# The second row's norm moved into the first row's last attention groups, with all unit and load places set anew

## The reference

```python
x = x + attn(layernorm(x))          # 16 heads of 32, linear attention in chunks, head-wise RMS norm
x = x + mamba(ctx, layernorm(x))    # conv, 16 states per channel, scan over 512 steps, gated by silu(layernorm(x))
x = x + ffn(layernorm(x))           # ternary weights (24 blocks of 128 x 1024), 8-bit activations
```

## Time and profile before

| | |
|---|---|
| three runs, median (lowest to highest) | 954.26 us (953.02 to 956.2) |
| the profiled execution | 954.95 us, span 953.2 us |
| busy: PE, DVE, ACT, POOL | 84%, 83%, 62%, 51% of the span |
| mean granted TensorE clock | 0.912 of full speed |
| row 0, step 1, step 2, step 3, last row | 213.7, 237.1, 217.4, 192.1, 92.9 us |

### The profile page before, as it was taken

The page is one execution under the profiler, slowest core; times in us unless marked ns, Lnnn a source line. Parts: engine busy times, 40 slices in busy tenths (PEclk is TensorE's granted clock), DMA queues, the critical chain, the costliest instruction groups (busy, mean ns, idle before and its releaser), DMA issues.

```text
span 953.2 us, 11602 instructions
## 1 busy us (share of the span) xinstructions
PE 804.4 (84%) x4036; PEld 445.1 (47%) x4036; DVE 787.1 (83%) x932; ACT 591.2 (62%) x865; POOL 481.7 (51%) x283
## 2 busy tenths in 40 slices
PE   5779678657688998998989788999978899998798
PEld 1336345433453444656354344656445346664354
DVE  5899976887687888979699998697599998977874
ACT  3779889974466766545367866455266787434443
POOL 0465776885536434574446653465455655562020
PEclk9789977858789899989989999989989999999799
DMA  9668887867336443775635673665724566673000
GB/s 292 247 180 250 221 250 215 243 189 210 77 66 138 98 99 67 178 155 129 148 66 100 121 145 67 145 144 111 177 66 89 111 149 130 150 158 66 1 12 34
DMA packets 50494, 130.92 MB, mean 137 GB/s; under 512 B 7203, under 2 KB 7587, under 8 KB 50437
## 3 DMA queue, kind: packets, MB, share of 16 engines
q0 software_dynamic: 16128, 58.73, 32.5%
q1 hardware_dynamic: 34308, 71.45, 24.1%
HBM read 67.09 MB, written 4.35 MB: 75 GB/s over the span
## 4 chain that ended last, share of the span: by engine, by line
PE 48%; DVE 21%; ACT 14%; issue 7%; DMA 6%; POOL 4%; SPq 0%; DVEq 0%; POOLq 0%; ACTq 0%
PE bank L847 15%; PE bank L1056 7%; DVE W L1842 5%; PE bank L970 5%; PE bank L876 4%; DMA ACC<-W 3%; PE bank L895 3%; PE bank L1073 3%; ACT DEC L1300 3%; PE bank L954 3%; POOL W L1680 2%; DVE U L1798 2%; DMA CROW<-c_rows 2%; PE bank L915 2%; PE bank L932 2%
## 5 line engine op out<-in xcount | busy, mean ns | idle before, releaser
L1680 POOL TENSOR_TENSOR W<-W,CROW 128x1024 f32<-128x1024 f32 x128 | 322.6, 2535 | 186.4 <-DVE W L1842 166.5
L1842 DVE TENSOR_TENSOR_SCAN W<-DEC,PB 128x1024 f32<-128x1024 f32 x125 | 285.1, 2281 | 7.6 <-DMA ACC<-W 3.9
L1693 POOL DMA_DIRECT2D ACC<-W x112 | 98.8, 882 | 152.3 <-DMA ACC<-W 127.6
L1831 DVE TENSOR_TENSOR PB<-DU,PB 128x1024 f32<-128x1024 f32 x128 | 156.6, 1224 | 19.4 <-PE PB L1011 17.8
L1300 ACT ACTIVATE DEC<-DT,ACOL 128x511 f32<-128x511 f32 x250 | 160.2, 709 | 7.4 <-DVE W L1842 7.3
L1056 PE MATMUL bank<-W,ARENA 128*128 128x512 fp8e4 x512 | 128.2, 396 | 0.0
L1255 ACT ACTIVATE ARENA<-bank 128x512 f32<-128x512 f32 x56 | 32.8, 591 | 86.0 <-PE bank L847 46.6
L1056 PEld LDWEIGHTS bank<-W,ARENA 128*128 128x128 bf16 x512 | 46.2, 100 | 64.9 <-issue 22.4
L876 PE MATMUL bank<-IDF,ARENA 128*128 128x128 f32 x384 | 56.5, 292 | 20.2 <-DVE ARENA L1861 9.5
L1398 ACT ACTIVATE ARENA<-bank,SDQ 128x512 f32<-128x512 f32 x64 | 43.3, 685 | 44.5 <-PE bank L1056 44.2
L1982 DVE SCALAR_TENSOR_TENSOR ARENA<-bank,SDQ,ARENA 128x512 f32<-128x512 f32 x64 | 47.4, 743 | 25.3 <-PE bank L876 9.5
(11 more groups left out here) (168 smaller groups left out, 1294.8 us busy)
## 6 DMA issues: line engine op xcount, KB each, us to landing
ACC<-W POOLq DMA_DIRECT2D x112, 512.0 KB, 4.7
CROW<-c_rows SPq DMA_DIRECT2D x98, 256.0 KB, 3.7
W<-in_wffn SPq DMA_DIRECT2D x27, 512.0 KB, 6.7
X<-in_wffn SPq DMA_DIRECT2D x21, 512.0 KB, 5.6
X<-in_x SPq DMA_DIRECT2D x7, 1024.0 KB, 8.0
out_dram<-X SPq DMA_DIRECT2D x16, 256.0 KB, 2.1
X<-in_ctxT SPq DMA_DIRECT2D x4, 512.0 KB, 5.7
ARENA<-in_x SPq DMA_DIRECT2D x1, 1024.0 KB, 5.8
```

Of the source, the lines that this page charges most:

```text
L1680: pool.tensor_tensor(w, w, CROW[k % 2][:, :].unsqueeze(1).broadcast_to([P, 2, L]), ALU.mult)\
L1693: pool.dma_start(ACC[accumulator(u)][:, :, :], w, accum_op=ALU.add).then_inc(y_summed, 16)
L1831: dve.tensor_tensor(into, du, rows, ALU.mult).then_inc(dbu_done.sem, 1)
L1842: dve.tensor_tensor_scan(flat(W[u % 4]), flat(decay_of(u)), flat(PB[:, scan_bank(u):scan_bank(u) + 2, :]), 0.0, ALU.mult, ALU.add).then_in ...
```

## The change

- `XROWS[1]` becomes X1 in place of X2. `norm_rows(1)` no longer waits for the last rounded weight block: it waits for `split(1)` and for the k features of group 0 in row 0, and is issued on SP's queue behind the C row of unit 15 (`ROW_ONE_AFTER = 13`).
- The norm of row 1 takes the same places in row 0's attention that the others have in rows 1 and 2: sums at the end of group 2, the rest in group 3. The q projection of row 1 becomes the first thing of step 1.
- `residual_rows(0)` (x[0] to X1) now waits until all four transposed blocks of row 1 are copied out, and is still issued behind the C row of unit 33.
- All tables are set anew. Pieces (of 256) done by the end of row 0, step 1, step 2, step 3: 66, 134, 195, 255 before; 65, 132, 192, 255 after. In row 0's last group there are 18 pieces (14 before), 11 weight blocks (9 before) and 7 decays (7 before); 6 of the blocks and 6 of the decays stand ahead of the four copies to XNT. By the end of group 2 of row 0, 47 pieces are done (52 before). The head of step 1 has 11 pieces (12 before); the heads of steps 2 and 3 have 6 and 8 before. The first loads of weights stand some units earlier (6 by unit 1, 4 before), those in the last third 1 or 2 later.

```diff
@@ all_products
-        if b > 1:
-            out += on(four, [(b, "q", 0)])
+        out += on(four, [(b, "q", 0)])
...
-        if b == 1:
-            out += on(four, [(b, "xnT", k) for k in range(KT)])
@@ tables: STEP_PIECES, STEP_DECAYS, STEP_SPREADS, STEP_SUMS, STEP_TERNS, STEP_LOADS, STEP_GAMMA
...
 STEP_TERNS, the last 14 places of row 0
-     (('a', 1, 2), 0), (('a', 1, 3), 4), (('a', 1, 4), 2), (('a', 1, 5), 1), (('a', 1, 6), 0), (('a', 2, 0), 1),
-     (('a', 2, 1), 1), (('a', 2, 2), 1), (('a', 2, 3), 1), (('a', 2, 4), 4), (('a', 2, 5), 1), (('a', 2, 6), 0),
-     (('a', 3, 0), 0), (('a', 3, 1), 2), (('a', 3, 2), 0), (('a', 3, 3), 1), (('a', 3, 4), 0), (('a', 3, 5), 2),
-     (('a', 3, 6), 4)],
+     (('a', 1, 2), 0), (('a', 1, 3), 3), (('a', 1, 4), 0), (('a', 1, 5), 2), (('a', 1, 6), 1), (('a', 2, 0), 0),
+     (('a', 2, 1), 1), (('a', 2, 2), 0), (('a', 2, 3), 1), (('a', 2, 4), 2), (('a', 2, 5), 3), (('a', 2, 6), 0),
+     (('a', 3, 0), 1), (('a', 3, 1), 2), (('a', 3, 2), 2), (('a', 3, 3), 1), (('a', 3, 4), 3), (('a', 3, 5), 1),
+     (('a', 3, 6), 2)],
...
+ROW_ONE_AFTER = 13
@@ buffers
-        XROWS = [part(2560, 2048).rearrange("p (t d) -> p t d", t=TT)] + [X2] * (BATCH - 1)
+        XROWS = [part(2560, 2048).rearrange("p (t d) -> p t d", t=TT), X1] + [X2] * (BATCH - 2)
@@ SP
             def residual_rows(b):
-                if b + 1 < BATCH:
+                if b == 0:
+                    for r in R.all_drained_at(*((1, "xnT", k) for k in range(KT))):
+                        sp.wait_ge(*r)
+                elif b + 1 < BATCH:
...
             def norm_rows(b):
                 if b == 1:
-                    sp.wait_ge(tern_done, WCH)
+                    sp.wait_ge(*bc_parts.at(1))
+                    sp.wait_ge(*R.drained_at(0, "k2", 0))
...
                 if j >= 0:
                     c_row(j + 2)
+                if j == ROW_ONE_AFTER:
+                    norm_rows(1)
...
             residual_rows(0)
-            norm_rows(1)
@@ PE, ACT and DVE: attention(b); the same edit at attention_products, normed_T, rstd, normed_columns, normed and rows_norm
-                    if b and b + 1 < BATCH and g == GROUPS - 1:
+                    if b + 1 < BATCH and g == GROUPS - 1:
@@ PE: step(b, f)
-                if b > 1:
-                    qk(b, "q", 0)
+                qk(b, "q", 0)
...
-                    if b == 1:
-                        for k in range(KT):
-                            normed_T(b, k)
-                    if b == 1:
-                        qk(b, "q", 0)
@@ ACT: step(b, f)
-                if b > 1:
-                    projection(b, 0, "q")
+                projection(b, 0, "q")
...
-                if b == 1:
-                    rstd(b, 0)
                 decays(b, "r", 3)
-                if b == 1:
-                    normed_columns(b)
                 if new:
-                    if b == 1:
-                        projection(b, 0, "q")
@@ DVE: step(b, f)
-                if b == 1:
-                    rows_norm(b)
...
-                if b == 1:
-                    normed(b, 0, XROWS[b], xn_ready)
```

More of the change, by code:

```diff
@@ L223, in all_products @@
         out += on(four, [(b, "dt", 2), (b, "dt", 3)])
-        if b == 1:
-            out += on(four, [(b, "xnT", k) for k in range(KT)])
         row = ffn_products(f, b)
-        out += on(four, [(b, "q", 0)] if b == 1 else []) + on(four, [(b, "k", 0), (b, "v", 0)])
+        out += on(four, [(b, "k", 0), (b, "v", 0)])
         out += on(every, [(f, "yT", t) for t in range(TT)])
@@ L2104, in attention @@
                     units(b, "b", g, 3)
-                    if b and b + 1 < BATCH and g == GROUPS - 2:
+                    if b + 1 < BATCH and g == GROUPS - 2:
                         rows_norm(b + 1)
```

## The result

The changed kernel takes 949.66 us (median of 20 runs, 946.99 to 954.75) against 952.98 us (20 runs, 946.78 to 956.2) for the kernel before on the same chip: a ratio of 0.9968, 95% interval 0.9953 to 0.9982, so 3 us less. A later job on another chip gave 950.41 against 954.69, 0.9946 (0.9926 to 0.9967). The profiled execution took 948.89 us, span 947.1; the one before had 954.95.

What follows compares the result with a forecast made beforehand. The prediction saw step 1's head bound by a chain leaving PE idle 14.07 us, through row 1's norm. Its terms, -14.5 + 4.0 - 1.5 = -12.0 against 954.95 us, gave 943 us, range 935 to 951.

Steps and rivals of the forecast that it cites:

- the hole: Head of step 1: PE idle 14.07 us until 246.06, released by DVE's normalisation of x[1]; the change takes this chain out.
- the range: Whole kernel: 935 to 951 us, taking in most forecast bounds, the port rival and two thirds of the second rival.
- the 943: Whole kernel: forecast time in us, 12.0 less than the profiled execution's 954.95; chance 0.62.
- 35.0 us, a saving of 14.5: Head of step 1: 35.0 us, sized by PE and DVE busy time; saving 14.5, bounds 10.0 to 15.7.
- the 40 us named as a sign of being wrong: Head of step 1: a length over 40 us would show the prediction wrong; 34 to 37 would show it right.
- I count it at nothing (bounds 0 and 8.6): SP's queue: moving the x[1] load behind unit 15's C row costs 0, as slack covers a late C row; bounds 0 and 8.6.
- 4.0 longer: Row 0: ACT's 3.0 us for the moved norm plus 1.0 for handovers; bounds 0 and 9.1.
- Row 0 gives most of it back: Row 0 rival, chance 0.15: last group 9 to 10 us longer, nothing returned earlier; 950.5 us.
- I take back 1.5 of it: Rest of step 1: without the hole PE's clock stays higher, 1.5 us less; bounds 0 and 4.0.
- 0, with bounds of 5 us either way: New places of pieces across rows and steps: what one saves another may pay, net 0, bounds 5 us either way.
- The port rival: Row 0 rival, chance 0.05: four normalisations wait behind POOL products on a shared port, up to 9.4 us growth; 948 us.
- The copies that hold the banks: Row 0's last group, rival, chance 0.07: PE's transposes wait 12 us for ACT's copies; +21.1, 961.5 us.

Runs made afterwards that it cites:

- a2: The changed kernel again, unchanged, as the base of two runs beside it on another chip; 950.41 us, ratio 0.9946 to the kernel before.
- e8: Changed kernel with a second 1024 KB load of x[1], to a spare HBM array, just ahead of the first; 952.82 us, ratio 0.9995 to before.
- e15: Changed kernel with the load of x[1] six units earlier and the places of rows 1 to 3 from before; 944.46 us, 0.9887 to before.
- e2: Kernel before with all seven new tables, the norm of row 1 left in step 1; 967.01 us, ratio 1.0145 to before.
- e9: Changed kernel with one scan of step 1 moved from between the last sums and their aggregation to behind the gate's shift; 949.04 us, 0.996.
- e12: Changed kernel with DVE's last mask of row 0 put ahead of four pieces; 949.73 us, ratio 0.9962 to the kernel before.
- e0: The kernel before, unchanged, in one more profiled execution for a second trace; 954.45 us.
- e16: Changed kernel with the early load, the later places of before and row 0's last square ahead of the last decay; 948.4 us, 0.9947 to before.

## Why the prediction was right or wrong

The direction and the mechanism were right: the hole is gone, and q covers part of the wait. The size was not. The forecast was 12.0 us less, and the medians give 3.3. The step that failed is the saving in step 1: 14.5 us for the head and 1.5 for the clock behind it, 16.0 together, where the traces show 9.7 (12.2 less in the head from the square, 2.5 more behind it). With it failed the load's cost, put at nothing, which likely is 1 to 3 us. That 949.66 still lies inside the range has two grounds other than the sum: the range was widened for the rivals, and the 943 was counted from a profiled execution 2.0 us above the median of the 20 runs, 952.98. Counted from that median the forecast would have been 941.0.

- **"35.0 us, a saving of 14.5."** By PE's mark the head takes 40.4, a saving of 9.1, just outside the bounds (10.0 to 15.7) and over the 40 us named as a sign of being wrong. By the last square it is 37.3, a saving of 12.2, and as long as step 3's 37.1. The value was taken by busy time, as if heads with equal work were equally long. PE's work was forecast at 30.8 and is 35.1. The 24 output projections take 12.23 us, against 10.54 in step 2 before; in step 3 before they took 12.23 too. This head has a granted clock of 0.88, step 2's 1.00, step 3's 0.90. In the second trace, a2, they took 10.54, but q 1.4 more. DVE's work was forecast at 25.7 and is 29.5: by the traces 11 pieces fall into this stretch before and after, so the 2.3 for "one piece" less was not saved, and NMR takes 1.4 more.
- **"I count it at nothing (bounds 0 and 8.6)", the load.** This step failed: a second load costs 3 us (e8), within the bounds. The text argued with the slack of C rows and W buffers, and C rows were not what it delayed. Taking zero needed a reason that covers the weight loads too, which stand behind it on the queue and for which ACT was seen to wait; the text had none. e8's wait of 7.15 us for weights is what it left out.
- **"4.0 longer", row 0.** +0.7 by PE's mark, +3.8 by the square, and 3.8 to 9.0 over the four traces. So the closeness of 3.8 to 4.0 is in part luck of two executions, all the more as the load's cost must be in it, which the 4.0 did not hold. The work of the last group was counted too low: its places in `STEP_TERNS` are 12 against 9, not two more, which is 11 scalings and 13 roundings of blocks against 8 and 9. That makes 3 x 1.23 + 4 x 1.14 = 8.3 us instead of 4.7. ACT's busy time in the group, up to PE's mark, is 41.5 us against 33.5.
- **"Row 0 gives most of it back" (0.15).** Its 950.5 us lies closest to the time measured, yet not by its mechanism alone: the last group is longer by 7.5 us to PE's mark and 10.7 to the square, but the groups before it give 6.9 back (1.9 to 6.9 over the four traces), which this rival excluded.
- **"I take back 1.5 of it", the rest of step 1.** +2.5, so 4.0 off, at the wrong side of the bounds (0 to -4.0). The clock did rise, 0.94 to 0.96. But DVE works 166.9 us there instead of 160.9: 28 scans and 28 products instead of 26 and 27. By PE's marks one of these three pieces stood in row 0 before and two in step 2; the head has none less. In e15, with the old places, the rest is 4.8 us shorter and the head 4.6 longer. And eight normalisations take longer:

```profile
L1776 DVE TENSOR_SCALAR X<-X,MV,RSTD 128x512 f32<-128x512 f32 x4 | 3.5, 946 | 0.0
L1776 DVE TENSOR_SCALAR OT<-X,MV,RSTD 128x512 f32<-128x512 f32 x4 | 2.5, 688 | 0.0
```

- **"0, with bounds of 5 us either way", the places.** Steps 2 and 3 cancel to 0.0. On the changed structure the later ones may cost 1 to 2 us, which three pairs don't settle; on the old structure all the new tables together cost 12 to 14 (e2). The price of a table depends on the structure it is for.
- **The port rival (0.05).** In row 0 it didn't happen: the four normalisations there take 2.02 us from 179.50. They fell between two POOL products (to 179.01, and from 182.46), so that the place is free is luck of this order and not shown for another. Elsewhere it did happen: 946 ns instead of 536, one of them 2.58 us, NMR 1.55 instead of 0.16, and L2043 3.40 for two in e9. The Trainium skill (SBUF — State Buffer, "Who interferes with whom") has, beside the rule for two-port modes that the prediction weighed, one for a DVE instruction with two SBUF inputs, which contends with a GpSimd instruction that reads SBUF. NMR and L2043 have two such inputs, and NMR ending 0.02 us behind POOL's product agrees. What the port cost was not in the place at which it was looked for, and the second rule hadn't been looked for at all. By estimate it is 1.4 us in the head (NMR) and 2.2 behind it (4 x 0.41 + 4 x 0.15); how much of that was on the path no run shows.
- **The copies that hold the banks (0.07).** Not seen: PE's transposes at 194.38 have no idle time ahead of them, and the four copies run on ACT from 196.13 in one go, 2.03 us.

By the trace the sum reads: -12.2 (head from the square) + 3.8 (row 0 with the load) + 2.5 (rest of step 1) = -5.9, where -12.0 stood. By the medians it is -3.3. The 2.6 us between them are the profiled executions' places in their scatter.

## What to carry to other kernels

A hole of 14 us is not worth 14 us. Once it is gone, the stretch is as long as the waits and the clock that are left: compare it with a stretch of the same program that is the nearest in granted clock too, not only in busy time. A table that was fitted to the hole is part of the change: new tables without the filled hole cost 12 us here. A transfer moved into a stretch in which weight loads already end waits has a price even where its own landing has 40 us of slack; bound it by every load behind it on the queue, and try its place, which here likely was worth some 3 us or more. And measure a step by the operation on which the next one depends, not by one engine's mark, and cut every kernel at that same mark.

## What the hardware showed that was not expected

- A DVE operation of 4 columns takes 0.16 us, or 1.55 us when a POOL product of 1024 columns is running, and ends with it. So it was in both traces of the changed kernel, in e8 and in e12.
- Two executions of the same program keep their distance to within 1 us over nearly 700 us behind row 0 (from +0.5 to -0.5 us before, 1.5 to 1.8 after), and come up to 3.7 apart within it. The head brings them closer by PE's clock, as far as e0 and a2 show, and not by idle time.
- e15 and e16 have the same tables behind row 0. From the start of step 2 to 483 us e16 is 2.7 us behind, at 486 us 0.5 behind, and from 526 us to the end 0.5 ahead. At 481 us begins a stretch of lower clock that only e15 has; first e15's lines, then e16's:

```profile
482.00:492.00 10.00, 10.00 (x54) 7.16 (x52) 9.08 (x17) 3.70 (x7) 1.47 (x2) 0.70 0.35 69
```

```profile
483.28 2.93 PE L918 MATMUL bank<-ARENA 128*128 128x128 f32 x12
```

```profile
482.00:492.00 10.00, 7.40 (x46) 4.85 (x46) 9.76 (x23) 5.66 (x11) 2.07 (x2) 1.00 0.62 130
```

```profile
485.10 1.61 PE L918 MATMUL bank<-ARENA 128*128 128x128 f32 x12
```

The 16 matmuls ahead of these 12 take 2.08 us in e15 and 1.16 in e16. So these 28 instructions at the lower clock (0.70 in the window, which is in part the level of 1.2 GHz, against 1.00) make up the 2.2 us; the rest comes later.
